# Source one-hots of 17 groups by ScalarE, and a front whose first projections take the weight's lower parts one by one

## The reference, cut to what matters

```
def t5_layer_norm(x, weight):
    var = mean(square(x));  return weight * (x * rsqrt(var + 1e-6))

def rgcn_conv(x, edge_index, edge_type, W_rel, W_root, bias):   # x [625, 1024], 20000 edges
    h_src = x[src]
    out = x @ W_root + bias                                     # W_root [1024, 286]
    for r in range(2):
        w = (edge_type == r)
        sums = segment_sum(h_src @ W_rel[r] * w[:, None], dst)  # W_rel[r] [1024, 286]
        cnt = segment_sum(w, dst)
        out = out + sums / max(cnt, 1)[:, None]
    return out

norm_x = t5_layer_norm(layernorm(x), ln_weight)
x = x + layernorm(x) + elu(rgcn_conv(norm_x, ...)) @ wo
x = x + ffn(layernorm(x))      # 8 experts, top 2 per row, and 2 shared experts
```

## Time and profile before

| | |
|---|---|
| median of three runs | 346.65 us |
| profiled execution, its own time | 347.6 us |
| its span in the trace | 345.9 us |
| busy share of the span: TensorE, VectorE, ScalarE, GpSimd | 93%, 68%, 38%, 21% |
| granted TensorE clock over the span | 1.00 |

### The profile page before, as it was taken

The page is one execution under the profiler, slowest core; times in us unless marked ns, Lnnn a source line. Parts: engine busy times, 40 slices in busy tenths (PEclk is TensorE's granted clock), DMA queues, the critical chain, the costliest instruction groups (busy, mean ns, idle before and its releaser), DMA issues.

```text
span 345.9 us, 5736 instructions
## 1 busy us (share of the span) xinstructions
PE 321.4 (93%) x1904; PEld 277.1 (80%) x1904; DVE 236.6 (68%) x461; ACT 131.2 (38%) x175; POOL 71.6 (21%) x91
## 2 busy tenths in 40 slices
PE   0799998888999999989998999999999999999995
PEld 0699897667789888878997888888888888878873
DVE  2999999996774582972746748665645656571994
ACT  2668142042013215161318655555644555530000
POOL 5643110000101101020022222342122320003840
PEclk9999999999999999999999999999999999999999
DMA  8960022000001015759122387499798992124994
GB/s 247 329 178 3 0 92 77 2 1 2 14 3 61 2 61 182 244 158 380 64 83 101 95 294 278 137 338 380 257 322 285 366 374 99 69 116 147 318 333 168
DMA packets 26753, 57.59 MB, mean 167 GB/s; under 512 B 2701, under 2 KB 16281, under 8 KB 26724
## 3 DMA queue, kind: packets, MB, share of 16 engines
q1 hardware_dynamic: 20198, 33.89, 29.0%
q0 software_dynamic: 3888, 14.16, 12.4%
q10 hardware_dynamic: 2638, 9.17, 6.8%
HBM read 66.25 MB, written 14.03 MB: 232 GB/s over the span
## 4 chain that ended last, share of the span: by engine, by line
PE 68%; DVE 12%; ACT 7%; issue 6%; DVEq 3%; DMA 3%; POOL 0%; SPq 0%; ACTq 0%
PE ps L1317 35%; PE ps L1582 16%; PE ps L1428 5%; PE ps L1572 4%; DVE work L963 4%; DMA raw<-in_L_gnn_W_rel 3%; PE ps L1327 2%; ACT arena_r L692 2%; DVEq L976 2%; DVE sw_raw L963 1%; PE ps L1463 1%; DVE big L973 1%; PE ps L1590 1%; ACT tile L699 1%; ACT arena_r L751 1%
## 5 line engine op out<-in xcount | busy, mean ns | idle before, releaser
L1317 PE MATMUL ps<-arena_r 128*128 128x512 f32 (+1 forms) x264 | 67.3, 401 | 0.2 <-DVE arena_r L1047 0.2
L1582 PE MATMUL ps<-big,tile 128*128 x272 | 61.7, 380 | 1.1 <-ACT tile L812 1.0
L1317 PE MATMUL ps<-arena_r,xt 128*128 128x286 f32 (+1 forms) x360 | 60.2, 311 | 0.3 <-ACT raw L708 0.3
L1317 PE MATMUL ps<-xt,arena_r 128*128 128x314 f32 (+2 forms) x312 | 59.6, 343 | 0.2 <-DVE xt L1038 0.2
L1582 PEld LDWEIGHTS ps<-big,tile 128*128 128x128 f32 x272 | 51.4, 190 | 9.3 <-issue 1.8
L1317 PEld LDWEIGHTS ps<-arena_r 128*128 128x128 f32 (+1 forms) x264 | 48.0, 188 | 11.0 <-DVE arena_r L1047 0.6
L1317 PEld LDWEIGHTS ps<-xt,arena_r 128*128 128x128 f32 (+1 forms) x312 | 50.2, 187 | 6.4 <-DVE xt L1038 0.4
L603 POOL DMA_INDIRECT big<-xrow,tok_i x17 | 31.6, 1857 | 99.7 <-PE ps L1572 75.4
L1317 PEld LDWEIGHTS ps<-arena_r,xt 128*128 128x128 f32 (+1 forms) x360 | 50.9, 194 | 1.2 <-ACT raw L708 0.5
L842 ACT ACTIVATE arena_r<-raw 128x2048 fp32r x17 | 32.5, 1910 | 26.7 <-DMA raw<-in_L_ffn_W 16.7
L1246 DVE TENSOR_TENSOR arena_r<-raw,arena_r 128x2048 fp32r<-128x2048 f32 x17 | 38.8, 2283 | 2.0 <-ACT arena_r L842 2.0
(11 more groups left out here) (210 smaller groups left out, 358.2 us busy)
## 6 DMA issues: line engine op xcount, KB each, us to landing
big<-in_L_ffn_W SPq DMA_DIRECT2D x19, 1024.0 KB, 7.7
raw<-in_L_ffn_W SPq DMA_DIRECT2D x19, 1024.0 KB, 10.2
yrow<-work ACTq DMA_DIRECT2D x17, 512.0 KB, 3.4
raw<-in_L_gnn_W_rel SPq DMA_DIRECT2D x2, 1144.0 KB, 12.0
y_acc<-in_x SPq DMA_DIRECT2D x4, 512.0 KB, 8.4
xrow<-work SPq DMA_DIRECT2D x4, 512.0 KB, 2.9
raw<-in_L_ffn_sW SPq DMA_DIRECT2D x2, 1024.0 KB, 5.9
sw_raw<-in_L_ffn_sW SPq DMA_DIRECT2D x2, 1024.0 KB, 12.5
```

The costliest lines, as they stand in the source:

```text
L1317: ins = pe.matmul(out_ap, a, b, start=start and k == 0, stop=stop and k == n - 1)
L1582: ins = pe.matmul(ps[1][:, i % 2, 0:HID], xg_t[:, k * P:(k + 1) * P], big[:, bass.ds(ring * UNIT + k * HID, HID)], start=k == 0, stop=k == ...
```

## The change

1. The source one-hots of the 17 odd groups 7, 9, ..., 39 are made by ScalarE: four activations Abs(iota − lo) into the four columns (`src_distance`), and one in place, Relu(1 − distance), over 512 elements (`src_hots`). VectorE makes only the key one-hot of these groups. `count` of such a group waits for `s_shot` too. `src_distance` of group g waits for count g − 8, whose buffer it takes.
2. `project` waits for each of the 8 lower parts of its weights by itself (`s_wlo`), in place of all 8.
3. Orders change. VectorE: stats 1 ahead of the edges; lower part of tile 2 ahead of stats 3; stats 4 from ahead of the loop into it, at g = 4; lower part of tile 1 ahead of stats 2. ScalarE: `centre(1)` to the second place; relation 1's upper part in two halves around `centre(2)`; `add_normed` of all tiles behind the loop's work. TensorE: transposes of tile 1 ahead of those of the edges; tile 4's at g = 10.
4. `LO_AT` becomes `{4: 3, 6: 2, 9: 8, 15: 3}`: statistics of tile 4, lower part of tile 3, lower part of W_root, lower part of tile 4.

```diff
-        LO_AT = {6: 3, 9: 10, 15: 3}
+        LO_AT = {4: 3, 6: 2, 9: 8, 15: 3}
+        ACT_HOT = tuple(range(7, G, 2))
...
             centre(0)
+            centre(1)
             split_rows(0, 0)
             act.wait_ge(s_bt, 1)
             act.activation(col_t[:, :], ps[2][:, 0, 0:NCOL], ACT.Copy).then_inc(s_colt, 1)
             act.wait_ge(s_colt, 1)
             weights_hi(0)
-            centre(1)
             split_rows(1, 1)
+            weights_hi(1, 0, KD // 2)
             centre(2)
-            weights_hi(1)
+            weights_hi(1, KD // 2, KD)
             split_rows(2, 2)
             weights_hi(2)
+            neg_lo = in_t
+            def src_distance(i):
+                g = ACT_HOT[i]
+                if g >= N_SH:
+                    act.wait_ge(s_cnt, g - N_SH + 1)
+                for c in range(CG):
+                    ins = act.activation(src_hot[g % N_SH][:, c // 2, :, c % 2], iota_s[0:CE, :, 0], ACT.Abs,
+                                         bias=neg_lo[:, g, c:c + 1])
+                ins.then_inc(s_dist, 1)
+            def src_hots(i):
+                act.wait_ge(s_dist, i + 1)
+                hot = src_hot[ACT_HOT[i] % N_SH]
+                act.activation(hot, hot, ACT.Relu, bias=1.0, scale=-1.0).then_inc(s_shot, 1)
+            def act_hots(first, last):
+                for i in range(first, last):
+                    src_distance(i + 1)
+                    src_hots(i)
             centre(3)
-            centre(4)
             h_out(0)
             split_rows(3, 3)
+            act.wait_ge(s_grp, 1)
+            act.activation(neg_lo, lo_t, ACT.Copy, scale=-1.0).then_inc(s_neg, 1)
+            act.wait_ge(s_neg, 1)
             h_out(1)
+            src_distance(0)
+            centre(4)
+            act_hots(0, 3)
+            h_out(2)
+            act_hots(3, 4)
             split_rows(4, 4)
-            act.wait_ge(s_rows, 1)
-            add_normed(0)
-            for t in range(2, T):
-                h_out(t)
-                add_normed(t - 1)
-            add_normed(T - 1)
+            act_hots(4, 7)
+            h_out(3)
+            act_hots(7, 15)
+            h_out(4)
+            act_hots(15, len(ACT_HOT) - 1)
+            src_hots(len(ACT_HOT) - 1)
             act.wait_ge(s_small, 32)
             act.activation(rw_hl[:, :, 0, :], rw_sb[:, :, :], ACT.Copy).then_inc(s_rw, 1)
             unit_hi(3)
             unit_hi(4)
+            act.wait_ge(s_rows, 1)
+            for t in range(T):
+                add_normed(t)
...
             stats_x(0)
+            stats_x(1)
...
-            stats_x(1)
             split_rows_lo(0, 0)
-            weights_lo(0)
+            dve.wait_ge(s_colt, 1)
+            weights_lo(dve, 0)
+            split_rows_lo(1, 1)
             stats_x(2)
-            split_rows_lo(1, 1)
             groups()
-            weights_lo(1)
+            weights_lo(dve, 1)
+            split_rows_lo(2, 2)
             stats_x(3)
-            split_rows_lo(2, 2)
-            stats_x(4)
...
             for g in range(G + LAG):
                 if g in LO_AT:
                     at = list(LO_AT).index(g)
-                    if at == 1:
-                        weights_lo(2)
+                    if at == 0:
+                        stats_x(4)
+                    elif at == 2:
+                        weights_lo(dve, 2)
                     else:
-                        split_rows_lo(3 + at // 2, 3 + at // 2)
+                        split_rows_lo(3 + at // 3, 3 + at // 3)
                 if g < G:
-                    hots(g, lo_t[:, g, :], v_t[:, g, :]).then_inc(s_hot, 1)
+                    hots(g, lo_t[:, g, :], v_t[:, g, :], g not in ACT_HOT).then_inc(s_hot, 1)
...
+            rows_t(xn, s_n, 1, 1)
             pe.wait_ge(s_const, 1)
             pe.wait_ge(s_kf, 1)
...
-            rows_t(xn, s_n, 1, 1)
             def project(t, r):
-                return hilo(ps[h_bank(t)][0:rows[t], r, 0:F],
-                            [((xt[:, 0, k, cols], xt[:, 1, k, cols]), (rel_hl[0][:, r, k], rel_hl[1][:, r, k]))
-                             for k in range(KD)])
+                for k in range(KD):
+                    pe.wait_ge(s_wlo[r], k + 1)
+                    ins = hilo(ps[h_bank(t)][0:rows[t], r, 0:F],
+                               [((xt[:, 0, k, cols], xt[:, 1, k, cols]), (rel_hl[0][:, r, k], rel_hl[1][:, r, k]))],
+                               start=k == 0, stop=k == KD - 1)
+                return ins
...
-                if g in (2, 8):
-                    t = 3 + g // 8
+                if g in (2, 10):
+                    t = 3 + g // 10
                     rows_t(xn, s_n, t, t)
                 pe.wait_ge(s_hot, g + 1)
+                if g in ACT_HOT:
+                    pe.wait_ge(s_shot, act_hots_upto(g))
```

More of the change, by code:

```diff
@@ L285, in program @@
         s_lo = sem("s_lo")
+        s_wlo = [sem(f"s_wlo{i}") for i in range(2)]
         s_v = sem("s_v")
@@ L301, in program @@
         s_hot = sem("s_hot")
+        s_neg = sem("s_negated")
+        s_dist = sem("s_distance")
+        s_shot = sem("s_srchot")
         s_cnt = sem("s_counted")
@@ L384, in raw_free @@
             def raw_free(n):
-                if not isinstance(n, int) or n >= 2:
-                    sp.wait_ge(s_lo, n - 1)
+                sp.wait_ge(s_wlo[n - 2], KD)
             def load_rel(n):
@@ L499, in unit_lo, with weights_lo @@
             eng.tensor_tensor(lo_v, raw_v, hi_v.bitcast(F32), ALU.subtract).then_inc(s_lo, 1)
+        def weights_lo(eng, n):
+            raw_v, hi_v, lo_v = gnn_units[n]
+            for k in range(KD):
+                eng.wait_ge(s_whi, n * KD + k + 1)
+                ins = eng.scalar_tensor_tensor(lo_v[:, k], raw_v[:, k], col_t[:, k:k + 1], hi_v[:, k].bitcast(F32),
+                                               ALU.mult, ALU.subtract)
+                if n < 2:
+                    ins.then_inc(s_wlo[n], 1)
+            if n == 2:
+                ins.then_inc(s_lo, 1)
         def far_loops(eng):
@@ L635, in steps_of, with act_hots_upto @@
             return h_steps[upto(g):upto(g + 1)]
+        ACT_HOT = tuple(range(7, G, 2))
+        def act_hots_upto(g):
+            return sum(1 for a in ACT_HOT if a <= g)
         def count_bank(n):
@@ L685, in unit_hi, with weights_hi @@
                 act.activation(hi_v, raw_v, ACT.Copy).then_inc(s_hi, 1)
-            def weights_hi(n):
+            def weights_hi(n, first=0, last=KD):
                 raw_v, hi_v, _ = gnn_units[n]
                 act.wait_ge(s_raw[n % 2], 16 * (n // 2 + 1))
-                for k in range(KD):
+                for k in range(first, last):
                     act.activation(hi_v[:, k], raw_v[:, k], ACT.Copy, scale=col_t[:, k:k + 1]).then_inc(s_whi, 1)
@@ L704, in h_out @@
                 act.wait_ge(s_h, t + 1)
-                act.wait_ge(s_lo, 2 if t < 2 else 3)
+                if t < 2:
+                    act.wait_ge(s_wlo[1], KD)
+                else:
+                    act.wait_ge(s_lo, 1)
                 if t in (0, 3):
@@ L922, in groups @@
                 dve.tensor_tensor(hr_t, hr_t, off_t, ALU.subtract).then_inc(s_grp, 1)
-            def weights_lo(n):
-                raw_v, hi_v, lo_v = gnn_units[n]
-                for k in range(KD):
-                    dve.wait_ge(s_whi, n * KD + k + 1)
-                    ins = dve.scalar_tensor_tensor(lo_v[:, k], raw_v[:, k], col_t[:, k:k + 1], hi_v[:, k].bitcast(F32),
-                                                   ALU.mult, ALU.subtract)
-                ins.then_inc(s_lo, 1)
             def stats_x(t):
@@ L947, in _, with hots @@
             dve.tensor_copy(d0_rows[:, :], ends[:, 0:1].to_broadcast([G, P])).then_inc(s_kf, 1)
-            stats_x(1)
             split_rows_lo(0, 0)
-            weights_lo(0)
+            dve.wait_ge(s_colt, 1)
+            weights_lo(dve, 0)
+            split_rows_lo(1, 1)
             stats_x(2)
-            split_rows_lo(1, 1)
             groups()
-            weights_lo(1)
+            weights_lo(dve, 1)
+            split_rows_lo(2, 2)
             stats_x(3)
-            split_rows_lo(2, 2)
-            stats_x(4)
-            def hots(n, lo, key):
+            def hots(n, lo, key, both=True):
                 def compare(hot, columns, index):
@@ L965, in compare @@
                         index.rearrange("p (q a c) -> p q a c", a=1, c=2).to_broadcast(shape), ALU.is_equal)
-                compare(src_hot[n % N_SH], iota_s, lo)
+                if both:
+                    compare(src_hot[n % N_SH], iota_s, lo)
                 return compare(key_hot[n % N_MH], iota_m, key)
@@ L1036, in split_lo @@
                 raw_v, hi_v, lo_v = unit_views(e, second)
-                dve.wait_ge(s_hi, (U_SW2 if second else U_SW1) + e + 1 - NLN)
+                dve.wait_ge(s_hi, (U_SW2 if second else U_SW1) + e + 3 - NLN)
                 dve.tensor_tensor(lo_v, raw_v, hi_v.bitcast(F32), ALU.subtract).then_inc(s_lo, 1)
@@ L1342, in _ @@
```

(10 more changed lines are left out.)

14 lines of the change are left out of this document (7 added, 7 removed).

## The result

The changed kernel takes 342.56 us (median of 4 runs, 341.08 to 343.78), the kernel before beside it 346.64. The ratio is 0.9868, 95% interval 0.9822 to 0.9914: faster by 1.3%. The gain is 4.1 us by the medians; between the two profiled executions it is 347.6 − 342.85 = 4.75 us, where 6.9 was forecast.

A forecast was written before the change was run, and what follows sets the result against it. VectorE's queue was taken as the bound from 8.14 to 82.35 us. Hole 0.76, one-hots 5.6, waits 0.5 and tile 4's statistics 1.56 − 1.56 sum to 6.9 us: 339.7 against 346.65, range 338.4 to 342.9.

The forecast's parts named there:

- likeliest case: Whole kernel: all terms of the sum come as forecast, 339.7 us, range 338.4 to 340.9; chance 0.68.
- hole 0.76: VectorE's front: tile 1's statistics fill the idle 1.38 us ahead of the edges, so later work comes 0.76 us earlier.
- tile 4's statistics 1.56: VectorE: 1.56 us of statistics leave the front and enter the loop at g = 4, nothing gained at VectorE's end.
- one-hots 5.6: Loop: 17 source one-hots of 0.33 us leave VectorE's queue, gaining 5.6 us; a pair of groups takes 1.85.
- waits 0.5: First groups of the loop: about 0.6 us of VectorE's waits for TensorE lie there; 0.5 gained, between 0 and 0.7.
- margin of 4 us: Loop: ScalarE's last one-hot is ready at 70.4, VectorE wants it at about 74.5.
- TensorE's front: Front: first block of 48 matmuls starts at 15.8, not 17.88, takes 8.53 us and ends at 24.3.
- the step about the waits one by one: TensorE's front: matmul steps never catch up with the lower parts, so waiting for each costs nothing; start at 15.8.
- Rival 3: TensorE's front: slow matmul pace ends at 22.4 as before, first block ends at 25.2; gain 5.8, 340.8 us; chance 0.12.
- Rival 2: ScalarE: Abs and Relu lie in another table, about 12 loads of 1.28 us, 15 us in all; 351 us; chance 0.03.
- Rival 1: Loop: ScalarE becomes the bound from 1.98 us per one-hot, slower kernel beyond 2.41; chance 0.08 short of that, 0.02 beyond.
- Rival 4: Loop: VectorE waits for TensorE's counts or `split_rows(4)`, losing one to three us of the gain; 342 us; chance 0.07.

The follow-up runs named there:

- r2: Kernel before plus only ScalarE's 17 one-hots, with `add_normed` behind them; front orders and `LO_AT` as before: 342.12 us, kernel before 347.02, ratio 0.9850.
- r3: Changed kernel with all one-hots back on VectorE, so the new front alone: 348.26 us, kernel before 347.02, ratio 1.0038.
- r7: r4 with source one-hots of groups 22 and 34 also on ScalarE (19), tile 2's output behind its fourth one-hot: 341.77 us, ratio 0.9841.
- r4: Changed kernel with GpSimd making the mask `before` ahead of its wait for the edges: 341.36 us, kernel before 347.02, ratio 0.9832.
- r6: r4 with each projection waiting for all 8 lower parts of its weights at once: 342.68 us, kernel before 346.89, ratio 0.9860.
- r10: r4 once more, unchanged, on another chip: 341.03 us, kernel before 347.40, ratio 0.9834.
- r8: r4 with the six clearings of `big` also moved ahead of GpSimd's wait for the edges: 343.31 us, kernel before 346.89, ratio 0.9879.
- r5: r4 with ScalarE's Relu of 512 elements cut into eight of 64: 346.07 us, kernel before 346.89, ratio 0.9971.
- r1: Changed kernel once more, no edit, as a control: 342.88 us, kernel before 347.02, ratio 0.9867.
- r9: r4 with group 34's source one-hot also on ScalarE (18), fifth Relu ahead of tile 4's upper part: 340.73 us, ratio 0.9813.

## Why the prediction was right and where it was not

The time came out 2.9 us above the 339.7 forecast, inside the range given (338.4 to 342.9), but outside the likeliest case's own range (338.4 to 340.9). The upper end of the range was made for rivals that didn't happen, and the time lies in it by 0.3 us because of two losses that the prediction didn't have, in `groups` and behind the loop: that much is luck. The profiled execution against the sum, by steps:

| step | forecast | measured |
|---|---|---|
| front: hole 0.76 and tile 4's statistics 1.56 | 2.32 earlier | 31.27 − 29.93 = 1.34 |
| loop: one-hots 5.6, waits 0.5, statistics −1.56 | 4.54 shorter | 51.08 − 46.66 = 4.42 |
| behind the loop | 0 | 264.5 − 263.55 = 0.95 longer |
| sum | 6.9 | 4.8 |

**The one-hots: right.** ScalarE needs 1.69 us for one where 1.74 was taken (an added Abs 0.29 as forecast, the Relu's addition 53.22 − 52.70 = 0.52 where 0.58 was taken). The pair takes 1.86 (forecast 1.85), and the term is worth 4.9 or 5.4 us by r2 and r3. What the prediction missed, without harm: `h_out` of tiles 2 to 4 waits for W_root's lower part, so ScalarE stood 1.92 us at 45.4, and another 1.23 for tile 4's transposes. The last one-hot was ready at 72.7 and not 70.4, so part of the margin of 4 us was used up, and the nineteenth one-hot of r7 found none left.

**The waits: 0.5 was taken, and about as much went, but not from where it was read.** Of VectorE's 1.8 us of waits for counts only 0.39 lay in the first groups (at 37.35); the 0.23 that the prediction put there too lay at 81.56. The 0.39 went, and so did 0.23 in which VectorE waited for ScalarE's upper part of row tile 3. 0.35 came anew between the first two groups (below).

**The hole: the mechanism was right and its 0.76 us were there, at 19.63; then they were lost in `groups`.** The step that failed is this one: "POOL's clearing of `big` starts 0.8 later, ends near 20.5 and is wanted at 32". It asked when the clearing is *wanted*, and took it that GpSimd's queue would be as long as before. It was 2.4 us longer, since the mask now lay beside a lower part; the clearing ended at 22.95 and not 20.5, beside `groups`. That costs 1.0 us in one trace of the kernel and 2.0 in the other, and turned a gain of 0.76 into a loss: r3 is 1.2 us slower than before, and r4, which moves the mask alone, has the gain back (first one-hot 29.21 and 28.79, forecast 28.95; last addition 75.87 and 75.46, forecast 75.4).

**TensorE's front: right in its end.** Forecast was a start at 15.8 and a block of 8.53 us; r4 has 15.77 and 8.78. In the trace of the kernel after it is otherwise:

```profile
12.62 1.47 PE L1395 MATMUL ps<-ident,work 40*125 40x40 f32 x12 [0.64 <-DVE d_rows L999]
...
14.36 8.16 PE L1371 MATMUL ps<-arena_r,xt 128*128 128x286 f32 x48
...
24.48 6.75 PE L1371 MATMUL ps<-arena_r,xt 128*128 128x286 f32 x48 [1.09 <-DVE arena_r L510]
```

The edges' transposes took 1.47 us and not the 2.71 of the earlier trace rows, the block started 1.4 us early, and TensorE then waited 1.09 for VectorE, late from `groups`. A TensorE that is early brings nothing there. The 1.47 stands in all three traces of the new front with the late mask, 2.71 in all seven with the early one; why isn't known. Waiting for all eight parts costs 1.3 us (r6), so the step about the waits one by one holds.

**Rival 3** (the slow matmul pace ends at 22.4) falls: it would end the block of the kernel after at about 24.3 from this start, and it ended at 22.52. The forecast's own rule, as many slow matmuls as before, doesn't hold either: the first block took 8.78 us in r4 and 8.22 in r10, which are the same kernel, 7.90 in r8 and 9.20 in r6. **Rival 2** falls with the two table loads. **Rival 1** is true of the mechanism, and its point was found (r5). **Rival 4** named the time that came, 342, by another way; in the loop VectorE waits for TensorE 1.4 us in 3 pieces, less than the 1.8 of the earlier trace rows, and loses nothing to it. Its idle time from 31 to 76 is about 0.8 us, below the 2 us that the prediction gave as a sign of being wrong.

**Behind the loop: wrong by the prediction's own sign.** It had the stretch unchanged at 263.5 us and named any other value as a sign of being wrong; it is 264.5, and 264.7 in r1. TensorE's landmarks that I compared (87.40, 98.46 and 168.06 before; 81.65, 92.71 and 162.31 after) are all 5.75 earlier, as the last addition is (5.76). One wait is new, in the chain of the kernel after:

```profile
235.72 0.96 issue
236.68 3.50 PE ps L1639 x15
```

Before, it is 0.11 us; in r1 1.10, in r2 0.42, in r7 1.16, in r8 0.31, in r3, r4, r5, r6, r9 and r10 none. The DMA engines are near their full share ahead of it, and which transfer is late wasn't found. r4 has all of the change and not the wait, so the moved work alone doesn't make it. But the two kernels that were traced twice show the same each time (0.96 and 1.10; none and none), so it isn't shown to be chance either: it may hang on when the stretch starts. r7 and r8 take some 1.3 us more still, and their chains end over the last gather (`big<-yrow`, 10.04 and 10.28 us), which ends no other run's chain. All this stays open.

**A small one that stays open.** Between the first and the second source one-hot of the loop lie 1.26 us in every kernel with the new front (the 0.35 before 31.19 in the timeline above) and 0.94 in the kernel before and in r2. That is 0.32 us that neither `groups` nor the stretch behind the loop explains. It wasn't tried.

## What to carry to other kernels

Where one engine's queue is the time of a stage, moving work from it to a slower engine that has room pays by what leaves the queue, not by what the slow engine needs: 5 us gained with one-hots that cost 1.69 us in place of 0.33. Find the cost at which the slow engine takes over (here 1.98), and how far it is away. When a reordering shifts two engines against each other by as little as 0.8 us, look for each GpSimd instruction at what it will then lie *beside* on VectorE, not only at when its result is wanted; moving one small mask was worth 1.2 to 1.5 us, in a kernel whose whole gain then was 5.7. And check the room that such a repair has: here it is 0.24 us.

## What the runs showed of the hardware

- A GpSimd mask of 128×128 float16 that reads SBUF took 0.28 us ahead of VectorE's lower parts (two sources in SBUF) and 2.65 us beside them, in three traces. The lower parts themselves weren't slowed: 3.49 us for eight, as in the earlier trace rows. Clearings by GpSimd, which only write, ran beside the same lower parts at their usual 0.94 us each.
- The same clearings hold up VectorE's casts and TENSOR_SCALARs with one source: a cast of 40 numbers stood for 0.69, 2.57 and 2.58 us in three traces (0.16 alone), a cast of 40×500 for 0.90 (0.41). The statistics of a row tile, which also have one source in SBUF, took 1.29 us beside them and alone, and copies out of PSUM 0.20 and 0.32 (0.19 and 0.31). What a collision costs isn't fixed by the program; the same kernel lost 1.0 and 2.0 us to it in two traces.
- The granted clock and TensorE's pace in the front don't go together. In the kernel after, busy with transposes from 12.62 on, it is 0.78 from 14 to 16, 0.50 (the lower level, 1.2 GHz) to 18, 0.87 to 20, and then 1.00. In the kernel before it is 1.00 (2.4 GHz) throughout, and yet from 18 to 22 the first block of 48 matmuls goes at 9 and 10 in 2 us, slower than the 11 of the kernel after at 0.50, and at 17 from 22 on, still at 1.00. The whole block takes 8.16 us in the one and 8.53 in the other. From the tables by windows (span and busy time of TensorE with its matmuls, granted clock, DMA share, GB/s), of the kernel after:

```profile
16.00:18.00 2.00, 2.00 (x11) 0.50 0.94 306
```

Of the kernel before:

```profile
18.00:20.00 2.00, 2.00 (x9) 1.00 0.78 170
```

- Eight ScalarE activations of 64 elements take 1.28 us where one of 512 takes 0.61.
